# A four-block attention and adapter kernel: its opening dealt anew over the issuing engines, with halves, masks first and shared weight splits

## The chip, the cores and the metric

One core of one Trainium2 chip runs the whole program. The metric is the device time of one execution in microseconds (us); the kernel before is given as the median of three runs.

## What is computed

For each of 32 batches `x` is a 256 x 256 matrix (256 tokens, 256 features) that goes through four residual blocks:

```
x = x + L0(x, side, lengths)   # 16 heads; q from side, keys and values from x with a length mask, and one own key per query
x = x + L1(x, language_id)     # h = relu(x@W1[id]+b1[id]); layernorm(x + h@W2[id]+b2[id]) * gamma[id] + beta[id]
x = x + L2(x, subject_id)      # x @ weight[id].T + bias[id]
x = x + L3(x, W1, b1, v, kind) # scores tanh(x@W1+b1)@v, masked softmax by kind of mask, pooled rows / count
```

All is fp32 in and out. A matmul that needs fp32 accuracy is made of three with operands that are split into a high part (fp32r) and a low part (what is left).

## The kernel before, in words

The program is written engine by engine, with a semaphore for each hand-over; nothing schedules it but the order of the code. It is a pipeline over steps `t = -2 ... 34`. In step t the batches t+2 (queries and keys are projected), t+1 (row scores for the maxima), t (key scores, exponentials), t-1 (attention's end, output projection), t-2 (adapter, linear) and t-3 (pooling, output) are at work together, each in its stage. `par` and `odd` name the two buffers of a pair.

For batch b the stage of t = b-2 makes `ss`, `xs` (split inputs), then q and k into PSUM; ScalarE copies them with a bias to `qf` and `kf`; they are split into `qp`, `kp` (in batch 0 into `aT` and `x1T`, whose own work comes later). Then DMAs spread them into the stacks `qst[par]` and `kst[par]`: 64 rows of a pair hold three 16-row pieces of the split, a row of the mask (`ONES`), and a row with the maxima (`MROW`). `stack_q` and `stack_k` each issue three DMAs for one half (four of the eight pairs of heads), `stack_q` also the mask row from the scratch tensor `mrow_d` in HBM. `maxima_put` issues four DMAs that write the negated maxima. `scores(pair)` of step t multiplies the stacks twice: key scores of batch t, which ScalarE exponentiates, and row scores of batch t+1, whose maxima VectorE takes (16 units a step). It waits for `stack0` or `stack1` (half 0 or 1 of batch t+1 in place) and `mput0` or `mput1`.

Steps -2 and -1 are the opening. In them the inputs and weights are loaded (`raw["q"]` and so on lie in the tile `pt`), the weights are split by VectorE (`split(n)`), the masks `hst` are made from the lengths (`leni`) and an index row (`kid`, in the tile `nv`), written to `mrow_d`, and read back from there. PE fills its waiting with matmuls of zeros on `hf`. `fold_load(j)` loads the j-th table of the linear block; the first five go to the tiles `yn`, `y` and three parts of `soft`. In steps 0 and 1 `fold_next` multiplies the eight tables by `w3`, into `lw3`; step 2 writes `lw3` to HBM (`lw3_d`) and each later step reads its subject's part from there into `lwf` (`linear_load`).

What was on the issuing engine SyncE (SP) runs in the order of its code, a wait holding up all behind it. ScalarE (ACT) issues DMAs as well, between its activations.

Of the kernel before, what the change touches and what calls it, by code (L numbers as in the profile page):

```python
# [42 lines left out]
P = 128  # L43
# [51 lines left out]
def block4(nc: bass.Bass, x, xsT, lens, ids, wq, wk, wv, wo, wad, lw, lwT, lb, fixed_d, early_d, kidx_d,  # L95
           pmask_d, out):
    ctx = ExitStack()
    with ctx:
# [162 lines left out]
        def stack_k(eng, half, b, par):  # L261

            pairs = slice(PH * half, PH * half + PH)
            eng.wait_ge(sem("ksplit"), done(b))
            low = x1T if isinstance(b, int) and b == 0 else kp
            for r in range(3):
                eng.dma_start(kst[par][r:P:EVERY, pairs, :].bitcast(F32),
                              low[r // 2][:, half, :].bitcast(F32)).then_inc(sem(f"stack{half}"), 16)


        @block.sync
        def _(sp):
            sp.dma_start(xsin[0][:, 1], xsT3[0, :, 1]).then_inc(sem("ld_xs0"), 16)
            sp.dma_start(xsin[0][:, 0], xsT3[0, :, 0]).then_inc(sem("ld_x0"), 16)
            sp.dma_start(kid, kidx_d).then_inc(sem("ld_kid"), 16)
            with nc.allow_non_contiguous_dma(reason="one length a row"):
                sp.dma_start(leni[:], lens).then_inc(sem("ld_kid"), 16)
            sp.dma_start(raw["v"], wv).then_inc(sem("ld_wv"), 16)
            sp.dma_start(xsin[1][:], xsT3[1]).then_inc(sem("ld_xs1"), 16)
            sp.dma_start(raw["o"], wo).then_inc(sem("ld_wo"), 16)  # L280
            sp.dma_start(early[:, 0:464], early_d).then_inc(sem("ld_early"), 16)
            sp.dma_start(btab[:, 0:D], lb).then_inc(sem("ld_early"), 16)
            sp.dma_start(idx[:], ids).then_inc(sem("ld_i"), 16)
            sp.wait_ge(sem("mask_split"), 2)
            sp.dma_start(mrow_d, mrows.bitcast(F32)).then_inc(saved, 16)
# [3 lines left out]

            def stack_q(half, b, par):  # L290

                pairs = slice(PH * half, PH * half + PH)
                sp.wait_ge(saved, 16)
                sp.wait_ge(sem("pool_set"), 4)
                sp.wait_ge(sem("qsplit"), done(b))
                sp.wait_ge(sem("st_ready"), done(b - 2, UNITS, UNITS // 2 * (1 + half)))
                if isinstance(b, int) and b == 1:
                    sp.wait_ge(sem("sn_ready"), 1 + UNITS // 2 * half)
                low = aT if isinstance(b, int) and b == 0 else qp
                for r in range(3):  # L300
                    sp.dma_start(qst[par][r:P:EVERY, pairs, :].bitcast(F32),
                                 low[r % 2][:, half, :].bitcast(F32)).then_inc(sem(f"stack{half}"), 16)
                sp.dma_start(kst[par][ONES:P:64, pairs, :].bitcast(F32),
                             mrow_d[bass.ds(b, 1), :].unsqueeze(1).to_broadcast([2, PH, S])).then_inc(
                                 sem(f"stack{half}"), 16)
# [10 lines left out]
            def fold_load(j):  # L316

                if j >= NLN:
                    sp.wait_ge(fold, j - NLN + 1)
                sp.dma_start(lwn[j % NLN], lw[j]).then_inc(ld_ln[j % NLN], 16)  # L320

            def step(t, par):
# [3 lines left out]
                def linear_load(su):  # L326

                    sp.wait_ge(sem("lwlo"), done(t - 3))
                    sp.dma_start(lwf[:, :, 0:D], lwT[su]).then_inc(sem("ld_lw"), 16)
                    sp.dma_start(lwf[:, :, D:NX], lw3_d[su]).then_inc(sem("ld_lw"), 16)  # L330

                if isinstance(t, int) and t == -2:
                    sp.wait_ge(saved, 16)
                    sp.wait_ge(sem("pool_set"), 3)
                    sp.wait_ge(sem("kst1_set"), 1)
                    for i in range(2):
                        sp.dma_start(qst[i][ONES:P:64, :, :].bitcast(F32),
                                     mrow_d[B:B + 1, :].unsqueeze(1).to_broadcast([2, PAIRS, S])).then_inc(sem("ones"), 16)
                        sp.dma_start(kst[i][MROW:P:64, :, :].bitcast(F32),
                                     mrow_d[B:B + 1, :].unsqueeze(1).to_broadcast([2, PAIRS, S])).then_inc(sem("ones"), 16)  # L340
                    stack_q(0, 0, 0)
                    stack_q(1, 0, 0)
                    for j in range(NLN):
                        fold_load(j)
                    sp.wait_ge(sem("ld_i"), 16)
                    return
                if isinstance(t, int) and t == 2:
                    sp.wait_ge(cat, SUBJ)
                    sp.dma_start(lw3_d.rearrange("j p c n -> p j (c n)"),
                                 lw3.rearrange("p j c n -> p j (c n)")).then_inc(lw3saved, 16)  # L350
                if on["F"] and not (isinstance(t, int) and t == 2):
                    su = which(1, t - 2, SUBJ - 1)
                    linear_load(su)
                if on["B"] and not (isinstance(t, int) and t == -1):
                    stack_q(1, t + 1, odd)
# [24 lines left out]
                if on["F"]:  # L380
                    if isinstance(t, int) and t == 2:
                        su = which(1, t - 2, SUBJ - 1)
# [3 lines left out]
                        linear_load(su)  # L386
# [3 lines left out]
                if isinstance(t, int) and t == 0:  # L390
                    fold_load(NLN)
                if on["A"]:
                    stack_q(0, t + 2, par)
# [3 lines left out]
                if isinstance(t, int) and t == 0:  # L397
                    fold_load(NLN + 1)
                    fold_load(NLN + 2)
# [11 lines left out]
        def _(pe):  # L411
# [19 lines left out]
            for _ in range(14):  # L431
# [31 lines left out]
            def step(t, par):  # L463
# [140 lines left out]
                if isinstance(t, int) and t == -2:  # L604
                    pe.wait_ge(sem("w_q"), 2)
                    queries()
                    pe.wait_ge(sem("w_k"), 2)
                    keys_()
                    return
                if isinstance(t, int) and t == -1:  # L610
                    own_keys()
                    queries()
                    pe.wait_ge(sem("ones"), 64)
# [6 lines left out]
                    free("v")  # L620
                    pe.wait_ge(sem("w_v"), 2)
# [8 lines left out]
                    return  # L630
                scores(0)
# [102 lines left out]
        def _(pool):  # L734
# [15 lines left out]
            def step(t, par):  # L750
# [13 lines left out]
                if isinstance(t, int) and t == -2:  # L764
                    ones(qst[1][:].bitcast(F32), 0.0, 3)
                    ones(mhalf[:], -0.5, 4)
# [99 lines left out]
        def _(act):  # L866
            def copy(dst, src, bias=0.0):
                return nc.scalar.activation(dst, src, ACT.Identity, bias=bias)  # L868

            act.dma_start(fixed[:], fixed_d).then_inc(sem("ld_fixed"), 16)  # L870
            act.dma_start(raw["q"], wq).then_inc(sem("ld_wq"), 16)
# [5 lines left out]
            def step(t, par):  # L877
# [60 lines left out]

                if isinstance(t, int) and t == -2:
                    own_high()  # L940
                    act.wait_ge(sem("ld_x0"), 16)
                    other_high()
                    act.wait_ge(sem("biases"), 3)
                    queries_out()
                    keys_out()
                    return
                if isinstance(t, int) and t == -1:
                    own_high()
                    other_high()
                    act.wait_ge(sem("pool_set"), 2)  # L950
                    stack_k(act, 0, 0, 0)
                    stack_k(act, 1, 0, 0)
                    queries_out()
                    keys_out()
                    act.wait_ge(sem("vaug_set"), 4)
# [102 lines left out]
        def _(dve):  # L1058
# [15 lines left out]
            for i in range(2):  # L1074
                nc.vector.memset(vaug[i][:, :, :, DH + 1:VW], 0.0).then_inc(sem("vaug_set"), 1)
                nc.vector.memset(vaug[i][:, :, :, DH:DH + 1], 1.0).then_inc(sem("vaug_set"), 1)
            for i in range(2):
# [4 lines left out]
            def split(n):  # L1082

                dve.wait_ge(sem(f"ld_w{n}"), 16)
                nc.vector.tensor_copy(W[n][0][:], raw[n]).then_inc(sem(f"w_{n}"), 1)
# [7 lines left out]
            nc.vector.memset(hst[B:B + 1, :].bitcast(F32), 1.0).then_inc(sem("mask_split"), 1)  # L1093
# [12 lines left out]
            def step(t, par):  # L1106
# [84 lines left out]
                if isinstance(t, int) and t == -2:  # L1191
                    dve.wait_ge(sem("xhi"), 1)
                    nc.vector.tensor_tensor(xs[0][1][:], xin[0], xs[0][0][:].bitcast(F32), ALU.subtract).then_inc(sem("xsplit"), 1)
                    dve.wait_ge(sem("qf"), 1)
                    dve.wait_ge(sem("qe"), 1)
                    nc.vector.tensor_copy(aT[0][:], qf[:]).then_inc(sem("qhi"), 1)
                    dve.wait_ge(sem("qhi"), 1)
                    nc.vector.tensor_tensor(aT[1][:], qf[:], aT[0][:].bitcast(F32), ALU.subtract).then_inc(sem("qsplit"), 1)
                    dve.wait_ge(sem("kf"), 1)
                    dve.wait_ge(sem("ke"), 1)  # L1200
                    nc.vector.tensor_copy(x1T[0][:], kf[:]).then_inc(sem("khi"), 1)
                    dve.wait_ge(sem("khi"), 1)
                    nc.vector.tensor_tensor(x1T[1][:], kf[:], x1T[0][:].bitcast(F32), ALU.subtract).then_inc(sem("ksplit"), 1)
# [192 lines left out]
```

## Time and profile before

| | |
|---|---|
| median of 3 runs | 961.24 us (960.85 to 963.36) |
| profiled execution, its own time | 958.85 us |
| its span, first to last instruction | 956.9 us |
| mean granted clock of TensorE | 0.979 |
| busy: PE, DVE, ACT, POOL | 96%, 73%, 67%, 64% of the span |

The span leaves out 1.95 us of the profiled execution's time; the profiled execution is itself 2.39 us below the median. All times of rows are microseconds from the start of the span. PE is TensorE's matmuls, PEld its weight loads, DVE VectorE, ACT ScalarE, POOL GpSimd; SPq and ACTq are DMA issues by SyncE and ScalarE.

### The profile page before, as it was taken

How to read it: one execution, taken by the hardware profiler on the slowest of the kernel's cores; microseconds unless marked ns; L12 is line 12 of the kernel's file. 1: busy time of each engine (PE TensorE's matmuls, PEld its weight loads, DVE VectorE, ACT ScalarE, POOL GpSimd, SP SyncE). 2: the span in 40 equal slices, each digit the busy share in tenths (PEclk: the TensorE clock that was granted, in tenths of full speed). 3: DMA queues.
4: the chain of work that ended last, by engine and by line, in shares of the span. 5: the costliest groups of instructions: out<-in, count | busy, mean ns of one | idle time of the engine just before them, and what ended most of it. 6: DMA issues, size and time to landing. Idle time of an engine off the chain costs nothing. (4 is left out here: it accounts for less than half of the span.)

```text
span 956.9 us, 27946 instructions
## 1 busy us (share of the span) xinstructions
PE 915.0 (96%) x8564; PEld 764.2 (80%) x8564; DVE 695.3 (73%) x1608; ACT 641.1 (67%) x1377; POOL 608.0 (64%) x771
## 2 busy tenths in 40 slices
PE   8899999999999999999999999999999999999855
PEld 7787788888888888888888888888888888877544
DVE  7765777877777778777777777777777777776442
ACT  2355677777677777776777777767777776677541
POOL 5333777767666777666676766666777676655551
PEclk9999999999999999999999999999999999999876
DMA  5544335344433444444334444443353444432311
GB/s 199 173 138 142 114 110 158 128 147 156 132 126 114 143 142 139 146 145 134 117 122 148 138 133 156 139 130 122 119 156 126 145 156 135 122 108 74 96 43 34
DMA packets 113193, 124.55 MB, mean 130 GB/s; under 512 B 23525, under 2 KB 95094, under 8 KB 113142
## 3 DMA queue, kind: packets, MB, share of 16 engines
q1 hardware_dynamic: 111846, 122.44, 40.5%
q10 hardware_dynamic: 1296, 1.46, 0.5%
q8 instruction: 27, 0.44, 0.2%
q14 instruction: 24, 0.20, 0.1%
HBM read 64.05 MB, written 8.96 MB: 76 GB/s over the span
## 5 line engine op out<-in xcount | busy, mean ns | idle before, releaser
L1132 DVE TENSOR_REDUCE mx<-SN 128x2 f32<-128x512 f32 x504 | 324.1, 685 | 72.4 <-PE SN L519 72.2
L890 ACT ACTIVATE pt<-ST 128x512 f32<-128x512 f32 x512 | 278.1, 599 | 81.1 <-PE ST L515 79.3
L515 PE MATMUL ST<-qst,kst 64*128 64x256 f32 x1024 | 187.9, 305 | 12.2 <-DVE mx L1132 4.5
L515 PEld LDWEIGHTS ST<-qst,kst 64*128 64x128 f32 x1024 | 136.1, 186 | 68.0 <-issue 26.4
L519 PE MATMUL SN<-kst,qst 63*128 63x256 f32 x1008 | 184.2, 305 | 0.1
L519 PEld LDWEIGHTS SN<-kst,qst 63*128 63x128 f32 x1008 | 132.8, 186 | 0.8 <-issue 0.4
L494 PE MATMUL PV<-pt,vaug 128*32 128x256 f32 x2048 | 125.1, 385 | 0.0
L748 POOL TENSOR_TENSOR ss<-xsin,ss 128x512 fp32r<-128x512 f32 x32 | 41.4, 1292 | 121.9 <-ACT ss L868 113.9
L494 PEld LDWEIGHTS PV<-pt,vaug 128*32 128x32 f32 x2048 | 60.4, 110 | 43.7 <-issue 6.6
L417 PE MATMUL M<-lwp,x2T 128*128 128x320 f32 x384 | 70.8, 321 | 1.0 <-DVE ob L1316 1.0
L748 POOL TENSOR_TENSOR x2T<-x2f,x2T 128x512 fp32r<-128x512 f32 x32 | 41.2, 1287 | 44.2 <-ACT x2T L868 44.2
L708 PE MATMUL M<-x,soft 128*128 128x256 f32 x256 | 65.6, 402 | 0.8 <-ACT soft L868 0.8
L748 POOL TENSOR_TENSOR xs<-xsin,xs 128x512 fp32r<-128x512 f32 x31 | 40.0, 1289 | 39.3 <-ACT xs L868 39.3
L791 POOL TENSOR_TENSOR nv<-nv,rec 128x512 f32<-128x512 f32 x32 | 34.0, 1062 | 43.2 <-DVE rec L1152 43.2
L417 PEld LDWEIGHTS M<-lwp,x2T 128*128 128x128 f32 x384 | 58.3, 193 | 1.8 <-DVE ob L1316 1.7
L417 PE MATMUL PV<-Wo,aT 128*128 128x256 f32 x384 | 56.6, 297 | 1.1 <-ACT pvt L868 1.1
L417 PE MATMUL PV<-ss,Wq 128*128 128x256 f32 x384 | 54.1, 291 | 1.9 <-POOL ss L748 1.9
L417 PE MATMUL M<-ss,Wk 128*128 128x256 f32 x384 | 55.3, 295 | 0.0
L868 ACT ACTIVATE qf<-PV,bqc 128x256 f32<-128x256 f32 x64 | 26.9, 471 | 42.4 <-PE PV L417 42.4
L708 PEld LDWEIGHTS M<-x,soft 128*128 128x128 f32 x256 | 49.5, 204 | 7.2 <-issue 1.1
L1161 DVE TENSOR_TENSOR x<-M,lbr 128x320 f32<-128x320 f32 x64 | 31.1, 486 | 32.2 <-PE M L417 32.2
L417 PE MATMUL M<-Wv,ss 128*128 128x256 f32 x384 | 53.8, 289 | 0.0
(140 smaller groups left out, 2088.1 us busy)
## 6 DMA issues: line engine op xcount, KB each, us to landing
qst<-qp SPq DMA_DIRECT2D x186, 128.0 KB
kst<-kp SPq DMA_DIRECT2D x186, 128.0 KB
xsin<-in_xsT SPq DMA_DIRECT2D x31, 512.0 KB, 3.4
adw<-in_wad SPq DMA_DIRECT2D x32, 322.5 KB, 3.9
pm<-in_pmask SPq DMA_DIRECT2D x32, 257.0 KB, 2.7
xr<-in_x SPq DMA_DIRECT2D x32, 256.0 KB, 4.2
lwf<-in_lwT SPq DMA_DIRECT2D x32, 256.0 KB, 3.1
out<-ob SPq DMA_DIRECT2D x32, 256.0 KB, 2.1
```

What stands on the lines that cost most here:

```text
L417: last = nc.tensor.matmul(dst, left(a, c), right(b, c), start=n == 0, stop=n == 5)
L494: last = nc.tensor.matmul(PV[32 * j:32 * j + 32, (g % 2) * S:(g % 2) * S + S], vaug[i][:, kb, 4 * g + j, :], pt[:, g, kb, j, :], start=kb ...
L515: keys = nc.tensor.matmul(ST[e][:, half * S:half * S + S], kst[par][lo_:lo_ + MROW + 1, pair, half * P:half * P + P], qst[par][lo_:lo_ + M ...
L519: rows_ = nc.tensor.matmul(rows_to[e][:, half * S:half * S + S], qst[odd][hi_:hi_ + MROW, pair, half * P:half * P + P], kst[odd][hi_:hi_ + ...
L708: last = nc.tensor.matmul(bank["pool"][:, i * D:i * D + D], p3T[:, c, i * P:i * P + P], x3[:, c, 0:D], start=c == 0, stop=c == 1)
L748: return nc.gpsimd.tensor_tensor(dst, src, high.bitcast(F32), ALU.subtract)
L791: nc.gpsimd.tensor_tensor(att[:].rearrange("p c (h d) -> p c h d", d=DH), nv[:].rearrange("p c (h d) -> p c h d", d=DH), rec[:].unsqueeze( ...
L868: return nc.scalar.activation(dst, src, ACT.Identity, bias=bias)
L890: nc.scalar.activation(pt[:, g, :, j, :], ST[s % 2][:].rearrange("p (h q) -> p h q", h=2), ACT.Exp, scale=SCALE).then_inc(sem("exp_done"), 1)
L1132: nc.vector.tensor_reduce(out=mx[odd][:, :, 8 * (s // 8) + PH * (1 - s % 2) + s // 2 % PH], in_=(ST if isinstance(t, int) and t == -1 and ...
L1161: nc.vector.tensor_tensor(x3[:, i, :], bank[f"lin{i}"][:, 0:NX], lbr[:], ALU.add).then_inc(sem("x3"), 1)
```

## The change

It touches the opening and the start of step 2.

The first loads are in another order: ScalarE issues the side input, Wq, the fixed constants and Wk; SyncE the lengths, the index row and the x input, two small ones, and only after the masks are made and sent to HBM the input of batch 1, Wv, Wo and the rest. VectorE makes the masks before any weight split, and clears `qst[1]` (which POOL did); the clearing of `vaug` moves behind the splits of batch 0. Of each weight split ScalarE makes the high part (`weight_high`), VectorE the low part. PE runs 8 filling matmuls, not 14. In step -2 the queries and keys of batch 0 come in halves, each in a bank of its own (PV, M1, M2, M0), and are copied and split by halves. SyncE issues both halves of batch 0's `stack_k` and the first half of `stack_q`; ScalarE issues the second half of `stack_q`, the first five `fold_load`s and the rows of ones of buffer 1. In step 2 `linear_load` comes first, with its `lw3` part read from SBUF and not from `lw3_d`.

```diff
         def stack_k(eng, half, b, par):
-            eng.wait_ge(sem("ksplit"), done(b))
+            first = isinstance(b, int) and b == 0
+            eng.wait_ge(sem("k0split" if first and half == 0 else "ksplit"), done(b))
...
+        def stack_q(eng, half, b, par):
+            eng.wait_ge(saved, 16)
+            eng.wait_ge(sem("st_ready"), done(b - 2, UNITS, UNITS // 2 * (1 + half)))
...
+            eng.dma_start(kst[par][ONES:P:64, pairs, :].bitcast(F32),
+            eng.wait_ge(sem("q0split" if first and half == 0 else "qsplit"), done(b))
...
         def _(sp):
-            sp.dma_start(xsin[0][:, 1], xsT3[0, :, 1]).then_inc(sem("ld_xs0"), 16)
...
             sp.wait_ge(sem("mask_split"), 2)
             sp.dma_start(mrow_d, mrows.bitcast(F32)).then_inc(saved, 16)
+            sp.dma_start(xsin[1][:], xsT3[1]).then_inc(sem("ld_xs1"), 16)
             sp.dma_start(raw["v"], wv).then_inc(sem("ld_wv"), 16)
...
-                    stack_q(0, 0, 0)
-                    stack_q(1, 0, 0)
-                    for j in range(NLN):
-                        fold_load(j)
+                    rows_of_ones(sp, 0)
+                    stack_q(sp, 0, 0, 0)
+                    stack_k(sp, 0, 0, 0)
+                    stack_k(sp, 1, 0, 0)
...
                 if isinstance(t, int) and t == 2:
                     sp.wait_ge(cat, SUBJ)
+                if on["F"]:
+                    su = which(1, t - 2, SUBJ - 1)
+                    linear_load(su)
...
-            for _ in range(14):
+            for _ in range(8):
...
                 if isinstance(t, int) and t == -1:
                     own_high()
                     other_high()
-                    stack_k(act, 0, 0, 0)
-                    stack_k(act, 1, 0, 0)
+                    weight_high("v")
+                    weight_high("o")
+                    stack_q(act, 1, 0, 0)
                     queries_out()
+                    for j in range(NLN):
+                        fold_load(act, j)
                     keys_out()
+                    rows_of_ones(act, 1)
...
             def split(n):
                 dve.wait_ge(sem(f"ld_w{n}"), 16)
-                nc.vector.tensor_copy(W[n][0][:], raw[n]).then_inc(sem(f"w_{n}"), 1)
                 dve.wait_ge(sem(f"w_{n}"), 1)
```

VectorE in the opening, before: the rows from the memsets to the end of batch 0's splits (`Wq1` is the low part of Wq, `aT` and `x1T` the splits of q and k).

```order
L1078 MEMSET mneg1 128x32
L1080 MEMSET rec 128x32
L1085 CAST Wq0<-pt 128x512
L1087 TENSOR_TENSOR Wq1<-pt,Wq0 128x512
L1091 CAST lenf<-leni 32x1
L1092 TENSOR_SCALAR hst<-nv,lenf 32x256
L1093 MEMSET hst 1x256
L1085 CAST Wk0<-pt 128x512
L1087 TENSOR_TENSOR Wk1<-pt,Wk0 128x512
```

The same place now:

```order
L1105 MEMSET rec 128x32
L1107 CAST lenf<-leni 32x1
L1108 TENSOR_SCALAR hst<-nv,lenf 32x256
L1109 MEMSET hst 1x256
L1110 MEMSET qst1 128x2048
L1116 TENSOR_TENSOR Wq1<-pt,Wq0 128x512
L1120 TENSOR_TENSOR xs01<-xsin0,xs00 128x512
L1116 TENSOR_TENSOR Wk1<-pt,Wk0 128x512
```

The masks stand ahead of the weights, the two casts are gone, and the clearing of `qst1` stands ahead of the first subtraction.

ScalarE in step -1, before: from the copies of batch 1's inputs to the values (`kst0<-x1T` are the key stacks of batch 0, `qf` and `kf` now batch 1's).

```order
L868 ACTIVATE xs10<-xsin1 128x512
L267 DMA kst0<-x1T0 32x4x256 x2
L267 DMA kst0<-x1T1 32x4x256
L267 DMA kst0<-x1T0 32x4x256 x2
L267 DMA kst0<-x1T1 32x4x256
L868 ACTIVATE qf<-PV,bqc 128x256 x2
L868 ACTIVATE kf<-M1,bkc 128x256 x2
L868 ACTIVATE vaug0<-M0 128x32x16
```

The same place now:

```order
L880 ACTIVATE Wo0<-pt 128x512
L279 DMA kst0<-mrows 2x4x256
L285 DMA qst0<-aT0 32x4x256
L285 DMA qst0<-aT1 32x4x256
L285 DMA qst0<-aT0 32x4x256
L880 ACTIVATE qf<-PV,bqc 128x256 x2
L299 DMA yn<-in_lw 128x512
L299 DMA y<-in_lw 128x512
L299 DMA soft<-in_lw 128x512 x3
L880 ACTIVATE kf<-M1,bkc 128x256 x2
L290 DMA qst1<-mrows 2x8x256
L292 DMA kst1<-mrows 2x8x256
```

Five table loads now stand between the copy of batch 1's queries and that of its keys.

SyncE behind the rows of ones, before (batch 0's query stacks, the tables, then batch 1's):

```order
L301 DMA qst0<-aT0 32x4x256
L303 DMA kst0<-mrows 2x4x256
L320 DMA yn<-in_lw 128x512
L320 DMA y<-in_lw 128x512
L320 DMA soft<-in_lw 128x512 x3
L368 DMA xsin0<-in_xsT 128x1024
L301 DMA qst1<-qp0 32x4x256
```

The same stretch now:

```order
L285 DMA qst0<-aT1 32x4x256
L285 DMA qst0<-aT0 32x4x256
L268 DMA kst0<-x1T0 32x4x256 x2
L268 DMA kst0<-x1T1 32x4x256
L268 DMA kst0<-x1T0 32x4x256 x2
L268 DMA kst0<-x1T1 32x4x256
L371 DMA xsin0<-in_xsT 128x1024
L279 DMA kst1<-mrows 2x4x256
L285 DMA qst1<-qp0 32x4x256
```

Six key stacks have come to SyncE, behind one half of the query stacks; the tables have left it.

## Rows read from the trace of the kernel before

**Rows 1.** The page: busy time of each engine, and the exponentials' group (mean ns).

```profile
PE 915.0 (96%) x8564; PEld 764.2 (80%) x8564; DVE 695.3 (73%) x1608; ACT 641.1 (67%) x1377; POOL 608.0 (64%) x771
...
L890 ACT ACTIVATE pt<-ST 128x512 f32<-128x512 f32 x512 | 278.1, 599 | 81.1 <-PE ST L515 79.3
```

**Rows 2.** Windows: stretch, busy of each engine, granted clock, DMA share, GB/s.

```profile
18.50:20.00 1.50, 1.36 (x9) 1.10 (x7) 1.47 (x3) 0.00 (x0) 0.24 (x1) 0.50 1.09 367
...
200.00:900.00 700.00, 692.41 (x6646) 579.04 (x6643) 530.32 (x1240) 504.64 (x1089) 474.25 (x606) 1.00 0.42 132
```

**Rows 3.** Timeline of step -2: start, us, engine and operation, [idle before it, releaser].

```profile
1.16 7.94 PE L432 MATMUL M<-hf 128*128 128x256 f32 x28 [1.16 <-DVE hf L1072]
...
1.48 1.76 DVE L1073 MEMSET kst<- 128x2048 f32 x1 [0.38 <-issue]
...
4.63 0.63 ACT L868 ACTIVATE ss<-xsin 128x512 fp32r<-128x512 f32 x1 [1.15 <-DMA xsin<-in_xsT]
...
6.24 2.45 DVE L1085 CAST Wq<-pt 128x512 fp32r<-128x512 f32 x1 [1.65 <-DMA pt<-in_wq]
6.60 1.81 POOL L737 MEMSET qst<- 128x2048 f32 x1
...
10.25 0.32 SPq L285 DMA_DIRECT2D mrows<-hst  x1
10.25 0.43 DVE L1085 CAST Wk<-pt 128x512 fp32r<-128x512 f32 x1
...
10.64 1.67 PE L417 MATMUL PV<-ss,Wq 128*128 128x256 f32 x12
...
11.69 0.70 SPq L337 DMA_DIRECT2D qst<-mrows  x1
12.39 0.84 ACT L868 ACTIVATE qf<-PV,bqc 128x256 f32<-128x256 f32 x2 [5.97 <-PE PV L417]
```

**Rows 4.** Timeline from batch 0's split to batch 1's keys.

```profile
13.72 0.69 DVE L1198 TENSOR_TENSOR aT<-qf,aT 128x512 fp32r<-128x512 f32 x1
...
14.57 1.91 SPq L301 DMA_DIRECT2D qst<-aT  x3
...
16.29 3.94 ACTq L267 DMA_DIRECT2D kst<-x1T  x6
...
17.47 2.34 PE L417 MATMUL PV<-ss,Wq 128*128 128x256 f32 x12 [1.91 <-POOL ss L748]
17.64 1.65 DVE L1087 TENSOR_TENSOR Wv<-pt,Wv 128x512 fp32r<-128x512 f32 x1
...
19.94 0.80 PE L519 MATMUL SN<-kst,qst 63*128 63x256 f32 x4
...
20.75 1.29 DVE L1132 TENSOR_REDUCE mx<-SN 128x2 f32<-128x512 f32 x2
21.04 3.13 SPq L320 DMA_DIRECT2D soft<-in_lw  x3
...
23.03 0.84 ACT L868 ACTIVATE kf<-M,bkc 128x256 f32<-128x256 f32 x2 [1.84 <-PE M L417]
```

**Rows 5.** Timeline up to the first scores and reductions of step 0.

```profile
24.77 1.28 POOL L748 TENSOR_TENSOR kp<-kf,kp 128x512 fp32r<-128x512 f32 x1
...
29.22 2.21 SPq L313 DMA_DIRECT2D qst<-mT  x4
...
32.69 0.35 PE L515 MATMUL ST<-qst,kst 64*128 64x256 f32 x1 [1.83 <-DMA kst<-kp]
...
33.29 1.27 DVE L1132 TENSOR_REDUCE mx<-SN 128x2 f32<-128x512 f32 x2
```

**Rows 6.** Timeline of step 2: GpSimd's wait for `lwf`, and two waits of PE.

```profile
95.74 0.87 POOL L798 TENSOR_TENSOR lwf<-lwf,fixed 128x128 f32<-128x128 f32 x2 [2.46 <-DMA lwf<-lw]
...
103.34 0.63 PE L425 MATMUL M<-fixed,yn 128*128 128x128 f32 x4 [1.03 <-ACT yn L1029]
...
104.70 1.70 PE L417 MATMUL PV<-Wo,aT 128*128 128x256 f32 x12 [0.73 <-ACT pvt L868]
```

More of the change, by code:

```diff
@@ L263, in stack_k @@
             pairs = slice(PH * half, PH * half + PH)
-            eng.wait_ge(sem("ksplit"), done(b))
-            low = x1T if isinstance(b, int) and b == 0 else kp
+            first = isinstance(b, int) and b == 0
+            eng.wait_ge(sem("k0split" if first and half == 0 else "ksplit"), done(b))
+            low = x1T if first else kp
             for r in range(3):
@@ L268, in stack_k @@
                               low[r // 2][:, half, :].bitcast(F32)).then_inc(sem(f"stack{half}"), 16)
+        def stack_q(eng, half, b, par):
+            pairs = slice(PH * half, PH * half + PH)
+            first = isinstance(b, int) and b == 0
+            eng.wait_ge(saved, 16)
+            eng.wait_ge(sem("st_ready"), done(b - 2, UNITS, UNITS // 2 * (1 + half)))
+            if isinstance(b, int) and b == 1:
+                eng.wait_ge(sem("sn_ready"), 1 + UNITS // 2 * half)
+            eng.dma_start(kst[par][ONES:P:64, pairs, :].bitcast(F32),
+                         mrow_d[bass.ds(b, 1), :].unsqueeze(1).to_broadcast([2, PH, S])).then_inc(
+                             sem(f"stack{half}"), 16)
+            eng.wait_ge(sem("q0split" if first and half == 0 else "qsplit"), done(b))
+            low = aT if first else qp
+            for r in range(3):
+                eng.dma_start(qst[par][r:P:EVERY, pairs, :].bitcast(F32),
+                             low[r % 2][:, half, :].bitcast(F32)).then_inc(sem(f"stack{half}"), 16)
@@ L326, in linear_load @@
                 def linear_load(su):
+                    first = isinstance(t, int) and t == 2
                     sp.wait_ge(sem("lwlo"), done(t - 3))
                     sp.dma_start(lwf[:, :, 0:D], lwT[su]).then_inc(sem("ld_lw"), 16)
-                    sp.dma_start(lwf[:, :, D:NX], lw3_d[su]).then_inc(sem("ld_lw"), 16)
+                    sp.dma_start(lwf[:, :, D:NX], lw3[:, bass.ds(su, 1)] if first else lw3_d[su]).then_inc(sem("ld_lw"), 16)
                 if isinstance(t, int) and t == -2:
                     sp.wait_ge(saved, 16)
[L334 to L340, printed above, removed]
-                    stack_q(0, 0, 0)
-                    stack_q(1, 0, 0)
-                    for j in range(NLN):
-                        fold_load(j)
+                    sp.wait_ge(sem("pool_set"), 2)
+                    rows_of_ones(sp, 0)
+                    stack_q(sp, 0, 0, 0)
+                    stack_k(sp, 0, 0, 0)
+                    stack_k(sp, 1, 0, 0)
                     sp.wait_ge(sem("ld_i"), 16)
@@ L630, in step @@
                     return
+                if isinstance(t, int) and t == 0:
+                    pe.wait_ge(sem("ones1"), 32)
                 scores(0)
```

135 lines of the change are left out of this document (69 added, 66 removed).

## The prediction

> **What bounds the kernel now.** The page first: PE is busy 96% of the span, no other engine over 80% [rows 1]. By windows, PE is busy 692.41 of the 700 us from 200 to 900 at full clock [rows 2]. So the steps in the middle are PE's own work, and the change does not touch them: what the opening gives is kept to the end. Then the timeline of the opening: PE multiplies the first scores of step 0 at 32.69, and VectorE starts its first reduction of step 0 at 33.29 [rows 5]. These two marks are what must move. Last, the timeline of step 2, where PE waits 1.03 and 0.73 us [rows 6].
>
> What sets the mark 33.29 is VectorE: from its first reduction of step -1 at 20.75 [rows 4] it works nearly without a hole, 12.54 us. What set 20.75 is the chain behind it: weight split, q, its copy at 12.39 [rows 3], stacks, and PE's queries of batch 1, which waited 1.91 us for GpSimd and took 2.34 [rows 4], against 1.67 for the same twelve matmuls before [rows 3], because the granted clock was at half (0.50, that is 1.2 GHz) in 18.50 to 20.00 [rows 2], after that wait. PE's mark 32.69 has a second chain: the copy of batch 1's keys ends at 23.87, GpSimd has split them at 26.05, SyncE issues three stacks, then the maxima's four DMAs from 29.22 to 31.43, and PE starts 1.26 us later [rows 4, 5].
>
> **The change, part by part: the weights and masks.** Before, the cast of Wq took 2.45 us beside GpSimd's clearing of `qst1` (6.60 to 8.41), while that of Wk took 0.43 [rows 3]. The casts go to ScalarE, which waited 5.97 us before its copy at 12.39 [rows 3]; a 512-wide copy there is 0.63 [rows 3]. VectorE gets the clearing instead, 1.76 us by the row of `kst` [rows 3].
>
> The masks are made first. The trace before has no row that says when such small loads land if they are first. Bounds: 4.63, when the first big load was in, and 6.24, when the third was [rows 3]. Being small and early they are nearer the first; I take 4.4. The masks then need 0.9 (from 8.69 + 0.69, the end of the Wq pair, to 10.25 [rows 3, 4]): 5.3. Now VectorE's order: clear 1.76, to 7.05; low part of Wq, of x, of Wk at 0.69 each [rows 4], to 9.15; three small biases, to about 9.5. PE's filling is 8/14 of 7.94 us, so it ends at 5.7 and is out of the way; the bias matmuls end by 7.7. The loads of Wq and Wk land as before or sooner (4.63, 6.24), since 1.2 MB now go ahead of the rest.
>
> **The halves.** PE needs 0.83 for six matmuls (half of 1.67), ScalarE 0.42 a half copy (half of 0.84) [rows 3], VectorE a half cast and subtraction 0.7 (no rows for halves; bounds 0.56 and 1.12, half and all of 0.43 + 0.69 [rows 3, 4]). The copies of q0, k0, q1 and k1 end at 10.0, 10.55, 11.4 and 12.25 (before: q whole at 13.23). The splits end at 10.75, 11.45, 12.15 and 13.0. Next on VectorE: clearing `vaug` (1,024 elements in four pieces: by the 1.76 of 2,048 it is 0.9, with four starts I take 1.1), to 14.1; the two products, 512 wide together, 0.9 (bounds 0.69, the subtraction, and 1.12), to 15.0; low parts of Wv and Wo, 0.69 each, of which one may suffer as before, 1.65 instead of 0.69 [rows 4], to 17.3; two small copies, to **17.7**, where the first reduction can start.
>
> Are the scores there by then? SyncE issues q's stacks 10.8 to 12.7 and k's to 14.6 (1.91 for three, [rows 4]); before, the last stack of half 0 was issued by 18.26 (half of 3.94 behind 16.29) and PE multiplied it at 19.94 [rows 4], so at most 1.7 later: 16.3. PE's queries: ScalarE's copy of the side input to 12.9, GpSimd's subtraction about 1.3 to 1.65, to 14.5, PE 1.67, to 16.2. Both are before 17.7, so their delays are covered by 1.4 us. VectorE is last: 20.75 - 17.7 = 3.05 us earlier. With the same 12.54 us behind it the first reduction of step 0 falls at 30.25, and PE's mark at **29.65**, 3.0 us earlier.
>
> **The queues.** ScalarE now issues eleven DMAs in step -1, before it was six. After 12.25: four high parts at 0.63 (two inputs, Wv, Wo), to 14.8; mask row and three stacks, 2.5, to 17.3; copy of batch 1's q, to 18.1; the five table loads. Before, the last three took 3.13 us on SyncE, one of them held up by about 2.2 us, the free ones 0.45 to 0.6 [rows 4]. Behind them on ScalarE stands the copy of batch 1's keys, and for that wait GpSimd's split, SyncE's key stacks and, behind these, the maxima. Free issues make 2.4 us: the copy ends at 21.4. Then 2.2 (split), 1.85 (three stacks, as queries'), 2.21 and 1.26 [rows 4, 5] give 29.0 for PE's mark. So ScalarE's issues lie beside VectorE's chain with 0.65 us of room; with it gone each further microsecond is on the path. The rows of ones of buffer 1, two issues behind that copy, land near 25, long before step 0 asks.
>
> The Trainium skill (DMA: Bandwidth & Descriptors, Issuing engines are not separate DMA queues) says that DMAs issued from several engines share the same 16 DMA engines, so that only issue time is saved. The trace agrees as far as it goes: 367 GB/s while both queues issued [rows 2]. By that rule the tables gain nothing by moving, and only their order counts.
>
> **Step 2.** GpSimd waited 2.46 us for `lwf`, and its late chain ended in PE's waits of 1.03 and 0.73 [rows 6]. The load now goes some 12 us earlier. Bounds: nothing and 1.76 us. The second wait is for two exponentials (0.6 each [rows 1]) and a copy of 0.6 behind the sixth scores, 1.75 in all, less the 0.63 of the transposes [rows 6]: 1.1 stays. I take 0.6 gained. The two loads and the write of `lw3` sit ahead of a stack that waits for scores anyway, so they cost nothing.
>
> **Sum.** 3.0 + 0.6 = 3.6 us off the profiled execution's 958.85: 955.25. The median is 2.39 above that execution, so the forecast for a median is 961.24 - 3.6 = **957.6**. About 0.3%, 2.9 us, is what a measurement of this kernel can tell from no change.
>
> **The rivals.**
> *The table loads stall on ScalarE.* If one of five is held as before, they take some 4.3 us, not 2.4; PE's mark is 30.9, the gain 1.8 + 0.6 = 2.4: 958.9, within 0.3%. For it: the row of 3.13. Against it: SyncE had more DMAs out then than ScalarE will have.
> *Late masks.* If the masks' loads land with Wq (6.24), all of VectorE's chain moves by 1.8: gain 1.2 + 0.6, 959.4, no change. A half clock in the halves' matmuls does the same for less.
> *More comes back.* No contention at Wv (0.95), the filling of `vaug` in a hole, and both waits of step 2 gone: PE's mark at 29.0, where the issues stop it, 3.7 + 1.76 = 5.4: 955.8.
> *Slower.* Each of the five loads is held by 2.2 us. Then they take 11, the keys' copy ends near 30, PE's mark is 37.5, 4.8 later than before; less 0.6 that is +4.2: 965.4. It turns slower by over 0.3% from a total of 9.6 us for the five on.
> *The first loads don't land sooner.* This is the late-mask case again and has its price.
>
> The skill's SBUF — State Buffer (Who interferes with whom) says that a VectorE instruction with two SBUF inputs and a GpSimd one that reads SBUF lock each other out for whole instructions. The row agrees at Wv (1.65 against 0.69 [rows 4]). By the rule both subtractions, Wv's and Wo's, could be held, one more 0.96 than I count, and the gain would be 2.6 us.
>
> **How the numbers follow.** Forecast 0.50 (own range 956.3 to 958.9, about a sixth of it above 958.35, the bound for faster); one stalled load 0.20; late masks or half clock 0.10; more 0.15; slower 0.05. Faster: 0.42 + 0.15 = 0.57. Same: 0.08 + 0.20 + 0.10 = 0.38. Slower 0.05. The range goes from the large gain, 955.8, to somewhat above late masks, 960.2.
>
> **What would show it.** First reduction near 17.7 and PE's first scores of step 0 near 29.7; the clearing of `qst1` on VectorE at about 5.3; five issues on ScalarE of 0.5 each and the copy of kf ending near 21.4; no wait of GpSimd for `lwf`, and no wait of PE for `yn` in step 2. Wrong would be: an issue of over 2 us on ScalarE, masks after 6, PE's mark later than 31, or a new half clock after step 0's start that takes back what was won.

## The result, and the profile after

The changed kernel takes 956.41 us in the median of seven runs (953.87 to 958.55), the kernel before 962.59 in seven (960.85 to 963.36). The ratio is 0.9942, 95% interval 0.9922 to 0.9961: 6.2 us less by the medians, 3.8 to 7.5 by the interval. Forecast were 957.6 in 955.8 to 960.2, which is 3.6 us less than the median then known, 961.24 of three runs. The time lies in the range; the gain was put too low, as the interval of the measured one starts at 3.8.

One row of the page after, which answers to [rows 1]:

```profile
PE 914.9 (96%) x8552; PEld 764.4 (80%) x8552; DVE 692.4 (72%) x1609; ACT 642.9 (67%) x1381; POOL 604.5 (63%) x770
```

PE's work is what it was. The timeline of the opening after, against [rows 3 to 5]:

```profile
1.16 6.49 PE L433 MATMUL M<-hf 128*128 128x256 f32 x16 [1.16 <-DVE hf L1100]
...
4.66 0.27 DVE L1109 MEMSET hst<- 1x256 f32 x1
...
5.42 1.76 DVE L1110 MEMSET qst<- 128x2048 f32 x1 [0.49 <-ACT Wq L880]
...
7.11 0.63 DVE L1116 TENSOR_TENSOR Wq<-pt,Wq 128x512 fp32r<-128x512 f32 x1
...
7.49 1.84 PE L439 MATMUL ST<-fixed,pt 128*128 128x1 f32 x16
...
9.19 0.96 PE L418 MATMUL PV<-ss,Wq 128*128 128x256 f32 x6
...
10.24 0.47 ACT L880 ACTIVATE qf<-PV,bqc 128x256 f32<-128x256 f32 x1 [2.31 <-PE PV L418]
...
15.35 1.16 DVE L1116 TENSOR_TENSOR Wv<-pt,Wv 128x512 fp32r<-128x512 f32 x1
16.43 0.68 DVE L1116 TENSOR_TENSOR Wo<-pt,Wo 128x512 fp32r<-128x512 f32 x1
17.03 0.35 DVE L1236 COPY x<-fixed 128x128 f32<-128x128 f32 x2
...
17.29 0.51 PE L520 MATMUL SN<-kst,qst 63*128 63x256 f32 x4 [0.76 <-issue]
...
17.80 1.29 DVE L1159 TENSOR_REDUCE mx<-SN 128x2 f32<-128x512 f32 x2 [0.42 <-PE SN L520]
...
29.38 0.35 PE L516 MATMUL ST<-qst,kst 64*128 64x256 f32 x1 [1.47 <-DVE mx L1159]
...
30.34 1.27 DVE L1159 TENSOR_REDUCE mx<-SN 128x2 f32<-128x512 f32 x2
...
32.91 2.93 PE L418 MATMUL M<-ss,Wk 128*128 128x256 f32 x12
```

The masks are done at 4.93 and not just before 10.25 [rows 3], VectorE's first reduction starts at 17.80 (forecast 17.7), PE's step 0 at 29.38 (29.65), VectorE's at 30.34 (30.25). So the two marks moved as worked out: 3.3 us for PE. (VectorE was ready for its first reduction at 17.38 and waited 0.42 us for the scores; why is told behind the experiments.) Yet the span of this execution is 956.0, only 0.9 less than before's. The windows after step 0's start say where the rest went; the columns are those of [rows 2]:

```profile
28.00:30.00 2.00, 0.62 (x8) 0.56 (x8) 1.86 (x5) 0.00 (x0) 0.00 (x0) 1.00 0.41 136
30.00:32.00 2.00, 0.36 (x5) 0.27 (x4) 1.58 (x5) 1.73 (x4) 0.15 (x1) 0.67 0.21 67
32.00:34.00 2.00, 2.00 (x13) 1.78 (x14) 1.29 (x2) 1.44 (x3) 1.12 (x1) 0.50 0.24 78
...
38.00:40.00 2.00, 2.00 (x13) 1.78 (x12) 1.29 (x2) 1.08 (x2) 0.00 (x0) 0.50 0.54 135
40.00:42.00 2.00, 2.00 (x16) 1.73 (x16) 0.22 (x1) 0.69 (x2) 0.00 (x0) 0.77 0.00 0
```

PE was idle for most of 28 to 32, then had work without a hole, at 0.50 of its clock (1.2 of 2.4 GHz) until past 40. Before, the clock was at half only from about 35 to 39 in its first trace. The marks of step 1's key matmuls tell the price: 59.05 before, 58.64 after. Of 2.56 us ahead in step 0 (35.47 against 32.91), 0.41 are left. Whether that belongs to the change or to chance, one pair of traces can't say.

### The profile page after: what moved, and what is told of

It is laid out like the page before. It is cut to its first block and busy times, and to the rows that moved or that the text cites. A ratio compares the mean times of both kernels' runs of the same rounds, so it can differ in the third digit from the quotient of the medians.

```text
span 956.0 us, 27862 instructions
## 1 busy us (share of the span) xinstructions
PE 914.9 (96%) x8552; PEld 764.4 (80%) x8552; DVE 692.4 (72%) x1609; ACT 642.9 (67%) x1381; POOL 604.5 (63%) x770
## 5 line engine op out<-in xcount | busy, mean ns | idle before, releaser
L418 PE MATMUL M<-Wv,xs 128*128 128x256 f32 x384 | 54.5, 292 | 0.1
```

Source lines behind the costliest of these rows:

```text
L418: last = nc.tensor.matmul(dst, left(a, c), right(b, c), start=n == 0, stop=n == 5)
```

## The experiments

Each kernel was timed against the kernel before, both on the same chip: r1 to r4 on one, r5 to r8 on a second, r9 to r12 on a third. The kernel before had medians of 960.82, 961.52 and 960.71 us there (960.54 beside r12), so a comparison of r3 with r5 to r12 is safer by the ratios. The times are medians with lowest and highest. The marks in the table are read from each profile: VectorE's first reduction, PE's first scores of step 0, and PE's key matmuls of steps 0, 1, 2 and 3.

| run | time | ratio to before (95%) | reduction | scores | key matmuls, steps 0 to 3 |
|---|---|---|---|---|---|
| before, first trace | 962.59 (960.85 to 963.36) | 1 | 20.75 | 32.69 | 35.47, 59.05, 86.77, 114.28 |
| after, first trace | 956.41 (953.87 to 958.55) | 0.9942 (0.9922 to 0.9961) | 17.80 | 29.38 | 32.91, 58.64, 86.36, 112.65 |
| r1 before again | 960.66 (957.84 to 963.59) | 1.0 (0.9982 to 1.0017) | 21.36 | 33.36 | 36.49, 60.59, 88.33, 114.61 |
| r2 after again | 955.82 (953.72 to 958.66) | 0.9954 (0.9934 to 0.9973) | 16.87 | 28.56 | 31.98, 55.71, 83.44, 109.72 |
| r3 after, filled | 953.56 (952.18 to 954.18) | 0.9925 (0.9902 to 0.9949) | 16.91 | 28.50 | 31.55, 53.74, 81.48, 107.76 |
| r4 before, filled | 957.53 (955.36 to 961.39) | 0.9964 (0.9948 to 0.998) | 20.47 | 33.54 | 36.20, 58.41, 86.12, 113.58 |
| r5 r3, `lwf` late | 953.87 (953.19 to 954.22) | 0.9921 (0.9906 to 0.9936) | 17.63 | 29.22 | 32.26, 54.45, 82.16, 109.45 |
| r6 r3, tables on SyncE | 953.21 (951.9 to 954.55) | 0.9917 (0.9901 to 0.9934) | 17.32 | 29.57 | 32.41, 54.59, 82.32, 108.61 |
| r7 r3, casts on VectorE | 954.65 (954.32 to 956.36) | 0.9936 (0.992 to 0.9952) | 18.70 | 30.27 | 33.31, 55.52, 83.25, 109.53 |
| r8 r3, loads as before | 956.52 (954.81 to 959.06) | 0.9955 (0.9937 to 0.9973) | 20.07 | 31.64 | 34.69, 56.89, 84.60, 110.88 |
| r9 r3, 14 fillings | 955.44 (954.94 to 955.91) | 0.9942 (0.9926 to 0.9958) | 19.30 | 30.89 | 33.94, 56.13, 83.87, 110.16 |
| r10 r3, `qst1` on GpSimd, 5 fillings | 956.03 (953.7 to 958.67) | 0.9946 (0.9927 to 0.9966) | 19.41 | 32.41 | 35.46, 57.67, 85.39, 111.67 |
| r11 r3, biases later | 953.24 (951.95 to 954.31) | 0.9917 (0.9899 to 0.9934) | 17.22 | 28.80 | 31.64, 53.85, 81.56, 107.86 |
| r12 r11, `qst1` on GpSimd | 951.88 (951.06 to 953.26) | 0.9909 (0.988 to 0.9938) | 17.22 | 28.80 | 31.64, 53.85, 81.58, 107.87 |

### Both kernels once more (r1, r2)

No edit.

> The kernel before, unchanged, for a second trace. Theory A (the clock's recovery after the start of step 0 varies from run to run and spreads the times of either kernel by 2 to 4 us): the half clock after step 0's start lasts otherwise than the 3 us of the first trace in some execution, and the execution's own time differs from 958.85 by about half of that difference, up to 963. Theory B (the times of the kernel are steady and the profiled run is simply less by a fixed amount): the half clock lasts 3 us again and the own time is within 0.5 us of 958.85.

> The changed kernel, unchanged. Theory A: its second trace has a half clock after step 0 that may last some 3 to 6 us and not 10; then the step marks stay 3 to 4 us ahead of before and the own time is 953.9 to 956.4. Theory B (the change itself prolongs the half clock): it lasts 10 us again, the own time is 958 again. The ratio to before is 0.992 to 0.996 under both.

Theory A held for the clock, and not for its price in r1. Before's second trace starts step 0 0.67 later than the first and is at half clock from 34 to over 40, about 6.8 us and not 3.4; by theory A its own time had to be higher for it, and it was 957.84, 1.01 less than the first's. It had gained elsewhere: 1.2 in step 2 and 1.1 at the end, as told below. After's second has the half clock from 28 to 35, 3.4 us shorter than its first, took 955.97 as theory A had it, and is 4.51 ahead of r1 in step 0 and 4.88 in step 1 (36.49 - 31.98, 60.59 - 55.71). The windows of r2:

```profile
28.00:30.00 2.00, 1.21 (x8) 0.95 (x8) 1.83 (x7) 0.52 (x2) 0.00 (x0) 0.65 0.50 168
...
34.00:36.00 2.00, 2.00 (x15) 1.93 (x13) 0.88 (x2) 0.00 (x0) 0.59 (x1) 0.64 0.82 261
36.00:38.00 2.00, 2.00 (x20) 1.87 (x20) 1.58 (x3) 1.09 (x2) 0.00 (x0) 1.00 0.44 112
```

So the same program spreads by some 5 to 6 us (957.84 to 963.59 in r1, 953.72 to 958.66 in r2), and a single profiled execution is a draw from that. A second spread is at the end, where PE waits in every step and the clock is at half for long stretches. From step 28's key matmuls (801.46 in the first trace) to the end of the span it is 155.44 and 154.32 in the two traces of before, 156.33 and 156.86 in those of after, and 154.3 to 156.9 over all. That takes 0.9 to 2.5 us back from after in these traces; whether it is chance is not settled, since r3 and r6, with the same code there, show 155.42 and 154.26.

### PE's idle stretches filled (r3, r4)

```diff
+            def fill(n):
+                for _ in range(n):
+                    nc.tensor.matmul(M[1][:, 0:S], hf[:, 0:P], hf[:], start=True, stop=True)
...
                     output_bias()
                     scores(7)
+                    pe.wait_ge(sem("kf"), 2)
+                    fill(3)
                     return
...
                 scores(0)
+                if isinstance(t, int) and t == 0:
+                    fill(3)
```

`fill(n)` is n matmuls of zeros. r4 has `fill(4)` in step -1 ahead of the queries, then `fill(3)` and `fill(2)` at the same places.

> The changed kernel with three matmuls of zeros in each of PE's two idle stretches around the start of step 0 (1.47 and 1.64 us idle). Theory A (the idle stretches let the clock fall, and the half clock costs half its length): the clock stays at 1.00 from 28 to 45 us, step 0's key matmuls take 1.7 and not 2.9 us, and the time falls by 3 to 5 us against the changed kernel in its long case, 1.5 to 3 in the median. Rival (the clock falls on VectorE's and ScalarE's pace, since PE is underfed in step 0 anyway): the half clock comes all the same and the time is within 1 us of the changed kernel; if a filler delays the scores, up to 1 us more.

> The kernel before with four filling matmuls of zeros in PE's wait of 1.9 us for the queries of batch 1, three before step 0 and two after its first scores. Theory A: no half clock in the opening; PE's queries take 1.67 and not 2.34 us, step 0's keys 1.7 and not 2.9, and the time falls by 1.5 to 3 us. Rival: as the opening is VectorE's chain, only what lies behind step 0's start counts, 1.2 us or less.

A row at step 0 of r3, and its windows:

```profile
29.16 1.56 PE L446 MATMUL M<-hf 128*128 128x256 f32 x6
...
31.55 1.69 PE L418 MATMUL M<-ss,Wk 128*128 128x256 f32 x12
```

```profile
30.00:32.00 2.00, 1.85 (x15) 1.31 (x14) 1.31 (x3) 1.50 (x5) 1.03 (x1) 1.00 0.03 4
32.00:34.00 2.00, 2.00 (x19) 1.94 (x17) 1.43 (x4) 0.99 (x2) 1.18 (x2) 1.00 0.54 180
```

The clock stays at 1.00, the key matmuls take 1.69 and not 2.93, and step 0 is 22.19 us long (31.55 to 53.74), not 25.73 (after's first trace) or 23.73 (r2). The median falls by 2.3 us against r2. r4 does the same for the kernel before: 3.1 us less than r1 by the medians, step 0 22.21 long. The rival fell in both. The clock fell near step 0's start in all four traces without the fillings, and from 28 to 48 it reads 1.00 in all ten with them (r3 to r12): it was the idle stretches that let it fall. What the fillings do to the spread is not settled. r3's six runs lie within 2.0 us where r2's ten lay within 4.9, but r4's twelve lie within 6.0, no less than r1's 5.8, and r10's six, with r3's fillings, within 5.0. In r4 the mean granted clock goes with the time, 0.984 at 955.36 and 0.978 at 961.39, so some executions lose it elsewhere; their traces were not kept.

With this fall of the clock out of the way, r3 is 3.97 us faster than r4 by the medians, and that is the best figure for what the change itself brings. The marks say more, 4.65 ahead in steps 0 and 1 and 5.82 in step 3, but they are one draw of each: the profiled execution of r3 took 952.18, its fastest, that of r4 958.79, 1.3 above its median. In r4 PE also waited 1.46 for a stack's DMA ahead of step 0, so that its scores stand 13.07 behind its first reduction, against 11.94 and 12.00 in the two traces of before; by the first reductions the lead is 3.56.

### Step 2 undone (r5)

```diff
-                if on["F"]:
+                if on["F"] and not (isinstance(t, int) and t == 2):
                     su = which(1, t - 2, SUBJ - 1)
                     linear_load(su)
...
                         sp.dma_start(lbs_d, btab).then_inc(lbsaved, 16)
+                        linear_load(su)
```

> The changed kernel with the fillers (as r3) and step 2's loads as before: lwf after the write to lw3_d and lbs_d. Theory A (step 2's order alone gives about 1.2 us): PE's waits for yn and pvt in step 2 are back at 1.0 and 0.7, step 3's key matmuls start 27.4 to 27.5 us after step 2's and not 26.3; time 1.2 us above r3's 953.6, 954.8. Rival (the order is worth 0.6, as predicted, or nothing): 954.2 or less.

PE's waits from 78 to 112 (us in total, times, longest), in r5:

```profile
PE ST L523 <- DVE mx L1170: 1.2, 2, 1.1
PE M L428 <- ACT yn L1068: 1.1, 1, 1.1
PE PV L420 <- ACT pvt L891: 0.7, 1, 0.7
```

and in r3:

```profile
PE ST L521 <- DVE mx L1168: 1.2, 2, 1.1
PE PV L418 <- ACT pvt L889: 0.8, 1, 0.8
```

From step 2's key matmuls to step 3's it is 27.29 us, against 26.28 in r3. So theory A held for the trace, with 1.0 us, and the rival for the time: the median is 953.87, 0.3 above r3's and inside the spread, and by the ratios there is no loss at all (0.9921 against 0.9925). With the change's order (r3) the wait for `yn` is gone and that for `pvt` is 0.8, where the prediction had nothing and 1.1. The kernel before doesn't always pay either. In r4 it did, 27.46 from step 2 to step 3; in r1 the row reads

```profile
95.98 0.87 POOL L798 TENSOR_TENSOR lwf<-lwf,fixed 128x128 f32<-128x128 f32 x2 [1.15 <-DMA lwf<-lw]
```

GpSimd waited 1.15 and not 2.46 [rows 6], because the load landed 3.5 us after its issue and not 4.8, and step 2 took 26.28 as after the change. The edit is worth 1.0 to 1.2 us at the marks of some executions and nothing in others; in the times no run shows it.

### The tables back on SyncE (r6)

```diff
                     stack_k(sp, 1, 0, 0)
+                    for j in range(NLN):
+                        fold_load(sp, j)
```

and out of ScalarE's step.

> As r3, but SyncE issues the five table loads, behind batch 0's stacks. Theory A (VectorE's chain sets step 0's start and the queue chain has some slack): the tables hold SyncE 2.5 to 4.5 us, the stacks of batch 1 and the maxima come later, but the keys' copy sooner; step 0 starts 0 to 1.5 us later than in r3, time 953.6 to 955. Rival (taking the tables off SyncE is what made the opening shorter): SyncE's chain is last by 3 us or more, time above 956.5.

The scores of step 0 come 12.25 us behind the first reduction and not 11.59; the time is the same, 953.21 against 953.56. The move of the tables is worth 0.7 us at that mark, as theory A had it, and not to be seen in the time. So SyncE's relief was not what shortened the opening. The Trainium skill (DMA: Bandwidth & Descriptors, Issuing engines are not separate DMA queues) says that issuing from several engines saves issue time alone; this run, no slower with the tables on one engine, agrees.

### The casts back on VectorE (r7)

```diff
                 dve.wait_ge(sem(f"ld_w{n}"), 16)
+                nc.vector.tensor_copy(W[n][0][:], raw[n]).then_inc(sem(f"w_{n}"), 1)
                 dve.wait_ge(sem(f"w_{n}"), 1)
```

and the four `weight_high` out of ScalarE's steps.

> As r3, but VectorE makes the high parts of the weights again (four casts). Theory A (VectorE is last all through the opening): every cast is on the path, 0.43 each and up to 0.7 beside GpSimd: the first reduction 1.6 to 2.2 us later, time 955.2 to 955.8. Rival (the copies' wait for loads or PE hides them): below 954.3.

The first reduction is at 18.70, 1.79 later than in r3 (16.91), the time 1.1 us more. The ranges of the two don't touch. The part is on the path, as theory A had it; the time shows somewhat less of it than was expected (954.65, not 955.2 or more).

### The first loads in the old order (r8)

```diff
-            sp.dma_start(kid, kidx_d).then_inc(sem("ld_kid"), 16)
             sp.dma_start(xsin[0][:, 0], xsT3[0, :, 0]).then_inc(sem("ld_x0"), 16)
+            sp.dma_start(kid, kidx_d).then_inc(sem("ld_kid"), 16)
...
+            sp.dma_start(raw["v"], wv).then_inc(sem("ld_wv"), 16)
+            sp.dma_start(xsin[1][:], xsT3[1]).then_inc(sem("ld_xs1"), 16)
...
             sp.wait_ge(sem("mask_split"), 2)
```

> As r3, but the first loads in the order of before, the two for the masks third and fourth on SyncE, all big ones ahead of the masks' wait. Theory A (masks first frees VectorE from 4.0 on): the masks' loads land near 6.3 and not 4.0, the clearing of qst1 and all behind it 1.5 to 2.3 us later, time 955.1 to 955.9. Rival (the high part of Wk and the bias matmuls set the start of the halves, which a later load does not move): below 954.3.

The masks' loads landed at 6.82, VectorE waited 3.33 us for them, and PE waited in turn:

```profile
6.82 0.14 DVE L1116 CAST lenf<-leni 32x1 f32<-32x1 int32 x1 [3.33 <-DMA leni<-in_lens]
...
10.57 1.65 PE L419 MATMUL PV<-ss,Wq 128*128 128x256 f32 x6 [1.23 <-DVE Wq L1125]
```

(`Wq L1125` is VectorE's low part of Wq.) The first reduction comes 3.16 us later and the time is 3.0 us more. That is more than the 2.7 us by which the masks are late (7.44 against 4.72): six matmuls that take 0.96 in r3 take 1.65 here, at a granted clock of 0.56 in the window from 10 to 12, after the wait of 1.23. Of the single parts this is the dearest, and dearer than theory A had it.

### Fourteen fillings again (r9), and fewer (r10)

r9 puts `range(14)` for `range(8)`. r10:

```diff
-            for _ in range(8):
+            for _ in range(5):
...
-            nc.vector.memset(qst[1][:].bitcast(F32), 0.0).then_inc(sem("qst1_set"), 1)
...
+                    nc.gpsimd.memset(qst[1][:].bitcast(F32), 0.0).then_inc(sem("qst1_set"), 1)
```

> As r3, but 14 filling matmuls at the very start, as before the change. Theory A (the filling stood on the path in both kernels: eight end at 6.3 to 7.65, fourteen at 9.1 to 10.1): the bias matmuls and all behind them move by six times 0.43, 2.6 us at most; what VectorE and the weight splits allow is 9.2 for the first q matmuls, so the first q matmul moves from 8.1 to about 10.7 and step 0's start by 2.0 to 2.6; time 955.6 to 956.2. Rival (as predicted, the filling is out of the way): no change, 953.2 to 953.9.

> As r3, but GpSimd clears qst1 again, behind its first subtraction, and five filling matmuls at the start, not eight. Theory A (from the masks to the first copy of q VectorE and PE are both late): VectorE's low part of Wq comes at 5.5 and not 7.1, that of Wk at 7.3, the bias matmuls end near 7.5 to 8; first reduction 0.7 to 1.2 us earlier; time 952.3 to 952.9. Rival (the loads of Wk and the halves' copies set the pace, or the clock falls with less filling): same as r3 or up to 1 us slower.

PE in the opening of r9:

```profile
1.16 8.00 PE L433 MATMUL M<-hf 128*128 128x256 f32 x28 [1.16 <-DVE hf L1109]
8.99 1.84 PE L439 MATMUL ST<-fixed,pt 128*128 128x1 f32 x16
10.70 0.96 PE L418 MATMUL PV<-ss,Wq 128*128 128x256 f32 x6
```

and of r10:

```profile
1.16 4.63 PE L433 MATMUL M<-hf 128*128 128x256 f32 x10 [1.16 <-DVE hf L1110]
6.15 3.57 PE L439 MATMUL ST<-fixed,pt 128*128 128x1 f32 x16 [0.35 <-DMA fixed<-in_fixed]
9.58 1.63 PE L418 MATMUL PV<-ss,Wq 128*128 128x256 f32 x6
```

r9 shows that the filling stood on the path: the reduction is 2.39 later, the time 1.9 more. The prediction had it "out of the way". Six fillings more end 2.58 us later than r3's eight (5.42 long), 0.43 each, while r10's first five take 4.63, 0.93 each: the fillings start slow and speed up. r10 shows the other side: after five fillings and a short wait the same bias matmuls take 3.57 and not 1.84, the first q matmuls 1.63 and not 0.96, about twice as long, and the first reduction comes 2.5 later. Between there and step 0 a half clock adds to that, though from 18.57 on PE had waited only once before it, 0.58 us (up to 21.94, for VectorE):

```profile
24.00:28.00 4.00, 4.00 (x25) 3.55 (x25) 3.02 (x7) 0.60 (x1) 1.35 (x2) 0.61 0.78 272
```

so the start of step 0 moves back by 3.9 us. Neither theory had that: A expected a gain, the rival at most 1 us of loss, and the time rose by 2.5. (The profiled execution took 957.83, 1.8 above r10's median, so that second part need not be in every run.) The granted clock's column reads 1.00 over all of r10's early rows, so in the first ten microseconds the durations have to be read and not the column. r10 changed two things at once; r12 parts them.

### VectorE's bias additions later (r11), and the best version (r12)

```diff
                     maxima_turn(1, t + 1, odd)
-                    output_bias()
                     return
...
                 unit(3)
+                if isinstance(t, int) and t == 0:
+                    output_bias()
```

r12 adds the clearing of `qst1` on GpSimd, with eight fillings.

> As r3, but VectorE's two bias additions (0.38 and 0.21) stand behind its first four reductions of step 0 and not ahead of them. Theory A (VectorE is last at step 0's start): the first reductions come 0.5 us earlier, PE waits less before its second scores, time 0.4 us less, 953.1. Rival (the maxima's DMAs are last): no change, 953.2 to 953.9.

> r11 with GpSimd clearing qst1 behind its first subtraction and the eight filling matmuls kept, which r10 had cut to five. Theory A (in r10 the shortened filling let the bias and q matmuls run at the slow rate and that cost 2 us, the clearing itself was an improvement): low part of Wk done near 8.4 and not 9.0, bias matmuls again 1.84 and not 3.57, first copy of q at 9.2 or earlier; first reduction at 16.7 to 17.3, time 952.7 to 953.3, no more than 0.5 us under r3, as PE's bias matmuls are then last. Rival (the clearing on GpSimd harmed r10): time above 954.5 and the first copy of q after 10.5.

r11 is r3 within its spread. At the marks theory A has its gain, about half of it: VectorE's first reduction of step 0 stands 0.54 behind PE's first scores and not 0.96, and from these scores to the key matmuls it is 2.84 and not 3.05 us. r12 clears r10's other edit: its bias matmuls take 1.84, its marks are those of r11 to 0.02 us, so the clearing is free on either engine, because VectorE's chain waits for Wk in either case. The sooner low part of Wq (5.51) brings nothing: ScalarE's copy of Wk starts at 6.84, as soon as it lands, in r11 too, and its copy of x stands behind it. Theory A had the first copy of q at 9.2; it was at 9.55.

```profile
6.84 0.63 ACT L890 ACTIVATE Wk<-pt 128x512 fp32r<-128x512 f32 x1 [1.43 <-DMA pt<-in_wk]
...
8.63 0.69 DVE L1125 TENSOR_TENSOR Wk<-pt,Wk 128x512 fp32r<-128x512 f32 x1
...
9.37 0.97 PE L418 MATMUL M<-xs,Wk 128*128 128x256 f32 x6 [0.21 <-DVE Wk L1125]
```

At 951.88 us (ratio 0.9909, 0.988 to 0.9938) r12 has the lowest median of all; its range (951.06 to 953.26) lies below all runs of both kernels, and overlaps with those of r11 and r3.

## Why the prediction was right, and where it was not

**What bounds it.** Right for the middle: from step 3's key matmuls to step 28's it is 687.18 and 686.97 us in the two traces of before, 687.02 and 687.22 in those of after. Not right up to the end, where after's two traces took 0.9 to 2.5 us longer. And one cause was read out of a single trace: that PE's queries of batch 1 ran at half clock because of the wait of 1.91. r1 has the same wait and no fall:

```profile
18.09 1.66 PE L417 MATMUL PV<-ss,Wq 128*128 128x256 f32 x12 [1.91 <-POOL ss L748]
```

and its first reduction came no sooner for it (21.36).

**The masks.** I took 4.4 for their landing; it was 4.04, and r8 shows that the order of loads is what brought it (6.82 with the old one).

**The weights.** Right in kind and size: the clearing took 1.76, the subtractions 0.63 to 0.69, low Wk was done at 9.26 (forecast 9.15). Undone alone (r7) the casts cost 1.79 at the mark.

**PE's filling.** The step "it ends at 5.7 and is out of the way; the bias matmuls end by 7.7" failed. I took 8/14 of 7.94; but the fillings do not run at one rate. Eight took 6.49 in the first trace, 5.42 in r3, and the bias matmuls ended at 9.33, as late as VectorE's low Wk (9.26); the q matmuls, whose low Wq was there at 7.74, stood behind them until 9.19. The first copy of q started at 10.24, not 9.6. That the mark came out at 17.80 all the same is luck: the later part of the chain was 0.6 shorter than I had it. Above all I had not seen that in the kernel before the filling, not the weights, came last ahead of q (7.94 from 1.16, then 1.84 of biases, then q at 10.64 [rows 3]), and that its length varies: 8.97 in r1.

**The halves.** Half casts took 0.29 and half subtractions 0.43, together the 0.7 that I took.

**Who is last.** "VectorE is last" failed, by little. I had PE's first scores of step -1 at 16.3, covered by 1.4 us; they started at 17.29, while VectorE was free from 17.38 on, and its reduction waited 0.42 for their end. The stacks' DMAs were late:

```profile
11.60 1.91 SPq L285 DMA_DIRECT2D qst<-aT  x3
...
13.55 3.85 SPq L268 DMA_DIRECT2D kst<-x1T  x6
```

SyncE began q's at 11.60 and not 10.8, as q's first half was late behind the filling, and k's for half 0 were issued by about 15.5 and not 14.6. r2, r3 and r9 have the same wait (0.35 to 0.39), while r7 and r8, with later casts or masks, have none: there VectorE is last.

**The contention.** I let one of two subtractions suffer by 0.96. Wv's took 1.16, Wo's 0.68: one suffered, by half of that. The Trainium skill (SBUF — State Buffer, Who interferes with whom) has a VectorE instruction with two SBUF inputs and a reading GpSimd one exclude each other; the rows agree for Wv, beside GpSimd's subtraction from 14.68 to 15.96, and Wo's began after that. In r12 it is Wq's that takes 1.06 and not 0.63, beside GpSimd's subtraction from 4.75 to 6.02.

**The queues.** No stall, as forecast, but the reason was partly wrong. I put ScalarE's issues in one line with its copies. In the trace they overlap:

```profile
12.55 1.11 ACTq L279 DMA_DIRECT2D kst<-mrows  x1
12.69 0.62 ACT L880 ACTIVATE ss<-xsin 128x512 fp32r<-128x512 f32 x1
...
14.36 1.40 ACTq L285 DMA_DIRECT2D qst<-aT  x2
...
17.53 1.91 ACTq L299 DMA_DIRECT2D soft<-in_lw  x3
...
19.68 0.47 ACT L880 ACTIVATE kf<-M,bkc 128x256 f32<-128x256 f32 x1 [2.27 <-PE M L418]
```

The mask row stands behind four copies in the program and its issue began before the first of them. The five tables were issued from 16.57 to 19.44, with no issue of 2 us, and the keys' copy waited for PE and not for them. The rivals "stall" and "slower" did not come about.

**Step 2.** Mis-sized: 0.6 taken, 1.2 in the first pair of traces (27.51 to 26.29), 1.2 between r4 and r3 (27.46 to 26.28), 1.0 in r5, nothing against r1.

**The sum.** 3.0 + 0.6 was made on one draw of either kernel. Over the two traces of before and five of after with its opening (first, r2, r3, r5, r11; the last three with fillings) the scores of step 0 start at 33.0 and 28.9 in the mean: the term of 3.0 measures 4.1. With about 1 for step 2 that is near 5, and the two comparisons gave 6.2 and 5.0 us by their medians, 3.97 with the clock held. The clock was in my list of what would make the forecast wrong, "a new half clock after step 0's start that takes back what was won"; it did so in the profiled execution, for 2.15 us, and does it to the kernel before as well. So for the profiled execution, on which the sum was worked out, it missed: 955.25 forecast, 958.23 taken. That the median came within 1.2 us of the forecast is in part luck too: the kernel before has a median of 962.59 in seven runs, 1.35 above the 961.24 that I took off from, and the gain was put 1.4 to 2.6 too low.

Left open: how the gain splits among the parts. Undone singly they bring back 1.79 (casts), 3.16 (loads) and 2.39 (filling) at the first reduction, 7.3 in sum, more than the whole change moves it; they cover one another. The halves by themselves were not tried, nor where the executions of r4 and r10 lose the time by which they still spread.

## What to carry to other kernels

Ask of matmuls that only fill time whether they end before the work that they precede: by a row, and not by a share of their number, since their rate changes while they run. Where PE waits for a microsecond or more before a long stretch of its own work, look at the clock behind the wait; if it fell, a few matmuls of zeros in the wait can hold it (here for 2.3 and 3.1 us of the medians). And where times of a program spread by more than the effect sought, read two traces of each kernel before a sum is made on one.

## What was not expected of the hardware

- The half clock after the idle stretches at step 0's start lasted 3.4 and 6.8 us in two executions of the kernel before, 10.2 and 6.8 us in two of the kernel after, and did not come when the stretches were filled (r3 to r12).
- Matmuls in the first ten microseconds ran at two rates under a granted clock that reads 1.00: sixteen bias records in 1.84 or 3.57 us.
- ScalarE's DMA issues did not wait for activations that stand ahead of them in the program, where no semaphore bound them: the issue at 12.55, the first of four activations ahead of it at 12.69.
- The same load of `lwf` from HBM let GpSimd wait 2.46 or 1.15 us in two executions of one program.
